# Layer 0 neighbour gather: a GpSimd queue drain behind every one of its 416 indirect DMAs

## The reference, cut to what matters

```python
xn = _layernorm(x)
msgs = edge_weight[:, None] * xn[edge_src]                # 50,000 x 256
agg = jax.ops.segment_sum(msgs, edge_dst, num_segments=3125)
h = (1.0 + eps[0]) * xn + agg
x = x + (jax.nn.relu(h @ w1 + b1) @ w2 + b2)
# then: routed experts, typed attention over the same edges, slice attention
```

## Time and profile before

| | |
|---|---|
| Median of 3 runs | 4517.4 us (4517.17 to 4521.95) |
| The profiled execution, its own time | 4514.77 us |
| Its span from first to last instruction | 4513.0 us |
| POOL busy over the span | 2876.4 us (64%) |
| PE busy | 2845.5 us (63%) |
| DVE busy | 2409.3 us (53%) |
| First gather to the end of the last gather | 592.7 us window |

### The profile page before, as it was taken

How to read it: one execution, slowest core, us unless ns; L and a number is a source line. 1 busy time by engine, 2 the same in 40 slices (tenths; PEclk the granted TensorE clock), 3 DMA queues, 4 the chain that set the end, 5 groups by cost and what they waited for, 6 DMA issues and landing times.

```text
span 4513.0 us, 51523 instructions
## 1 busy us (share of the span) xinstructions
PE 2845.5 (63%) x13735; PEld 1923.5 (43%) x13735; DVE 2409.3 (53%) x5005; ACT 1721.4 (38%) x4345; POOL 2876.4 (64%) x2661
## 2 busy tenths in 40 slices
PE   4200005545473990767777778996777777996698
PEld 1000003333362660224444447884444445885455
DVE  6434434444451114336777775556777776665353
ACT  2222310000021112125555556774555555885451
POOL 4777776666667887665555557996555553555640
PEclk5555556777785995777777778997777778997798
DMA  5444449333345653677676676777887765664300
GB/s 163 134 136 127 141 116 245 91 93 93 89 90 191 196 183 101 212 220 215 202 212 207 203 191 163 204 193 190 208 210 208 209 203 141 173 173 131 102 1 29
DMA packets 805880, 720.83 MB, mean 160 GB/s; under 512 B 424290, under 2 KB 700364, under 8 KB 805469
## 3 DMA queue, kind: packets, MB, share of 16 engines
q1 hardware_dynamic: 645116, 399.08, 31.1%
q0 software_dynamic: 153536, 315.11, 25.1%
q10 hardware_dynamic: 6944, 3.34, 0.3%
HBM read 482.09 MB, written 241.99 MB: 160 GB/s over the span
## 4 chain that ended last, share of the span: by engine, by line
DVE 20%; POOL 16%; another core or an unknown queue 12%; PE 12%; issue 9%; ACT 7%; DVEq 4%; ACTq 2%; DMA 1%; SPq 1%; POOLq 0%
POOL rec_src L564 9%; DVE META L1423 7%; POOL AR L1661 4%; DVE BIGR L648 3%; DVE AR L1443 3%; ACT AR L1717 2%; DVEq L1439 2%; DVE AR L639 2%; DVE AR L1436 2%; ACT AR L1719 1%; ACT AR L1547 1%; PE ps L1822 1%; PE ps L2433 1%; ACTq L1718 1%
## 5 line engine op out<-in xcount | busy, mean ns | idle before, releaser
L1392 POOL DMA_INDIRECT AR<-kv_tab,META x832 | 791.0, 951 | 599.8 <-DVE AR L1436 337.0
L536 POOL DMA_INDIRECT rec_dst<-AR,slot_e x400 | 484.6, 1211 | 166.7 <-issue 166.4
L1423 DVE TENSOR_REDUCE META<-ps 128x8 f32<-128x1024 f32 x416 | 507.7, 1221 | 97.9 <-remote 57.7
L668 PE MATMUL ps<-AR 128*128 128x256 f32 x832 | 305.6, 532 | 362.4 <-issue 151.0
L622 POOL DMA_INDIRECT AR<-xn_tab,META x416 | 397.9, 956 | 199.7 <-issue 128.6
L1661 POOL TENSOR_TENSOR AR<-AR 128x896 f32<-128x896 f32 x208 | 352.1, 1693 | 233.3 <-ACT AR L1726 230.4
L1626 DVE TENSOR_TENSOR BIGR<-BIGR,ps 128x260 f32 x832 | 353.6, 425 | 228.9 <-PE ps L1700 144.6
L1700 PE MATMUL ps<-AR 128*128 128x260 f32 x1664 | 419.5, 395 | 11.3 <-POOL AR L1661 5.4
L1521 PE MATMUL ps<-AR,identb 128*128 128x512 bf16 x832 | 405.4, 487 | 15.4 <-issue 8.5
L564 POOL DMA_INDIRECT rec_src<-AR,slot_e x290 | 351.8, 1213 | 91.8 <-issue 88.3
L668 PEld LDWEIGHTS ps<-AR 128*128 128x128 f32 x832 | 212.8, 268 | 456.1 <-issue 262.3
(11 more groups left out here) (432 smaller groups left out, 5815.7 us busy)
## 6 DMA issues: line engine op xcount, KB each, us to landing
v_dst<-AR SPq DMA_DIRECT2D x104, 384.0 KB
AR<-v_dst SPq DMA_DIRECT2D x104, 384.0 KB
v_src<-AR SPq DMA_DIRECT2D x104, 384.0 KB
AR<-v_src SPq DMA_DIRECT2D x104, 384.0 KB
AR<-in_W_qvk SPq DMA_DIRECT2D x44, 608.0 KB
rec_raw<-AR SPq DMA_DIRECT2D x40, 640.0 KB, 3.3
AR<-rec_dst SPq DMA_DIRECT2D x104, 192.0 KB
AR<-rec_src SPq DMA_DIRECT2D x104, 192.0 KB
```

The source lines that it names most:

```text
L536: pool.indirect_dma_start(rec_tab[0], bass.IndirectOffsetOnAxis(ap=slot_e[0][0:EP, c * CC + k:c * CC + k + 1].bitcast(U32), axis=0), RD[s] ...
L668: ins = pe.matmul(l0_ps(s, u), OW[s][:, u, :], GA[s][:, u, :], start=True, stop=True)
L1392: pool.indirect_dma_start(KVR[s][:, u, 0:KV], None, kv_tab, bass.IndirectOffsetOnAxis(ap=META[o][:, g * U + u, 0:1].bitcast(U32), axis=0)) ...
L1423: ve.tensor_reduce(BMALL[o][:, g * U + 2 * half:g * U + 2 * half + 2, :].rearrange("p b h -> p (b h)"), PSA[:, 2048 + 1024 * half:3072 + 1 ...
```

## The change

`pool.drain()` is put behind each indirect DMA of `l0_pool`, inside the loop over the four blocks of a group. That is 416 drains in all. A drain on an engine's queue holds back what follows it on the same queue until the engine has finished what stands ahead of it. No instruction changes its place, no wait, buffer, semaphore or size changes, and all other stages and engines keep their code.

```diff
@@ -622,6 +622,7 @@
                     pool.indirect_dma_start(GA[s][:, u, :], None, xn_tab,
                                             bass.IndirectOffsetOnAxis(ap=META[0][:, g * U + u, 0:1].bitcast(U32), axis=0)
                                             ).then_inc(sem(f"rows{s}"), 16)
+                    pool.drain()
 
         def l0_vector(ve):
             ve.tensor_tensor(X[:, 0:N2, :], X[:, 0:N2, :], b2x.unsqueeze(1).to_broadcast([P, N2, D]), ALU.add)
```

## The result

The changed kernel takes 5444.2 us (median of 4 runs, 5433.7 to 5451.8) against 4517.6 us before. The ratio is 1.205, with an interval of 1.202 to 1.207. I had forecast 4640 us, with a range that ended at 4705. The time lies at rival B, which I had priced at 5427 us and given a chance of 0.05.

The account below looks back on a forecast made before the run. POOL's gather issue was taken to set the stage's pace, 5.0 of 5.7 us a group. Stage +128.9 us, less 5.4 at its end, on 4514.8 gave 4638.3, stated as 4640 us; range 4595 to 4705.

Parts of the forecast that it names:

- rival B: Drain waits until the gather has landed, gap 2.68 us between POOL's gathers, whole 5427 us; chance 0.05.
- the price of a drain between gathers: On POOL in the gather stage, each gap between gathers grows from 0.30 to 0.78 us; 415 gaps make 323.7 us.
- work ahead: POOL's queue prepares the next gather while the present one runs, starting it 0.30 us after; a drain ends that.
- the sum's 721.6: Forecast gather stage on POOL: 397.9 us busy plus 323.7 us of gaps, against 592.7 us before.
- The price of lost preparation: Next gather on POOL is prepared only after the present one finishes; gap 0.78 us instead of 0.30.
- My sum: Whole-kernel forecast: 128.9 us more for the gather stage less 5.4 at its end, +123.5 us.
- The pauses: POOL's waits for late PE increments in the gather stage, 70.3 us, all to be given back at the slower pace.
- Rival A: POOL's pauses stay despite the slower gathers; up to +55 us, 4695 us, or 4710 with all of it; chance 0.10.
- The end of the stage: POOL resumes 6.3 us after the last gather instead of 11.75, which gives back 5.4 us.
- What follows: Everything after the gather stage starts later by the same time; it costs nothing more and hides nothing.
- The cover: DVE's and PE's 2.8 to 2.9 us per group lie well inside POOL's 6.9 us in the gather stage.

Follow-up runs that it names:

- e3: Kernel before, with a POOL wait for each gather's own landing and a drain behind that wait; 5487.4 us, ratio 1.207.
- e1: Kernel before, with a tiny POOL memset behind each gather and a wait for its semaphore, no drain; 4562.2 us, ratio 1.0035.
- e5: Changed kernel, drains kept, with gathers of 256-byte rows instead of 1 KB; 4929.4 us, ratio 1.206 to the kernel before.
- e6: Changed kernel, drains kept, with gathers of 2 KB rows, each for two blocks; 4457.0 us, ratio 1.091 to the kernel before.
- e7: Kernel before, with a tiny memset, a wait for its semaphore and a nop behind each gather, no drain; 4691.8 us, ratio 1.039.
- e4: Kernel before, with one drain behind the fourth gather of each group only, 104 in all; 4750.6 us, ratio 1.045.

## Why the prediction was wrong

**The step that failed** is the price of a drain between gathers. I bounded it by rows in which work ahead had finished, and took "finished" to be the gather's recorded end. A gather's record ends 1.81 us before its last increment lands, and the drain waits for the landing. e3 (113 ns with nothing in flight), e1 (engine free 0.11 us after the record) and e5 with e6 (the drain follows the length of the transfer) show it. The gap was 2.7 us on average and not 0.78. The stage came to 1522.6 us and not to the sum's 721.6. These 801 us are nearly the whole error of 5444 - 4640 = 804 us.

**The rule that I let weigh too much** is that of the Trainium skill, "PSUM — Partial Sum Buffer", "Engine vs sequencer instructions": a drain waits for the engine to go fully idle. I read it as leaving transfers out. No row spoke for that reading, and with no row on either side a chance of 0.05 was far too low. In these runs POOL's drain counts its own indirect DMAs in flight. It doesn't count those of SP's queue: the zero fills took 14.4, 27.8 and 42.7 us to land, and no drain beside them was longer than 7.5 us. Other engines' drains were not tried.

**Rival B's sum was right.** It took 1.90 us from the earlier trace rows and 0.78 from the earlier trace rows, gap 2.68, whole 5427 us. Measured were a gap of 2.7 and 5444 us. That they agree so closely is partly luck. B's parts are a little long: a single gather's gap in the quiet part of the stage is 2.6 us (1.88 + 0.70). What brings the mean up are the 20 early gathers with slow landings, which B did not price.

**The price of lost preparation was right** where nothing has to land. Behind a drain the next gather starts 0.70 us later, and e7, which has that price without a landing, has 0.75. My sum with e7's memset added is 123.5 + 415 x 0.12 = +173 us; measured were 4691.8 - 4515.8 = +176. The 50 ns that the Trainium skill, "DMA: Bandwidth & Descriptors", section "Anatomy of one DMA — SWDGE (gpsimd) path", gives for the dispatch would have made it far less. By the gaps of 0.75 us in e7 it isn't the time from release to start of a DMA that the queue had not prepared.

**The pauses went,** as forecast: no remote wait is left on POOL, and DVE's adds follow PE's products by 0.14 us. Rival A was wrong. Their 70 us were a gain inside a loss of 930.

**The end of the stage** gave back 11.75 - 7.18 = 4.6 us, forecast 5.4. What follows kept its length, as forecast.

**The cover held.** PE's and DVE's work per group stayed far inside POOL's pace, 14.6 us a group now. PE's rose from 2.9 to 383.2 / 104 = 3.7 us, at a mean granted clock of 0.56 instead of 0.73, and that cost nothing.

## What to carry to other kernels

Behind an indirect DMA on POOL, a drain costs the DMA's whole way to its landing plus the start of the next DMA from nothing: here 2.7 us on top of the engine's 0.95 us of work. To hold the next DMA only until the engine is free, let a tiny POOL instruction increment a semaphore and let the next DMA wait for it (0.38 us between gathers). To order the data, let the DMA that needs it wait for the landing semaphore, which was 0.4 to 0.5 us cheaper for each gather than the drain and can be put several DMAs later, as PE's wait for four gathers is in this kernel. A nop between a wait and a DMA costs nothing while the wait is met early (0.30 us gaps in the kernel before), and some 0.5 us where the queue stands at the wait.

## What the runs showed of the hardware that I had not expected

PE's semaphore increments seem to reach all waiting engines up to 15 us late while POOL issues indirect DMAs back to back. In this stage POOL's pauses came to 69.6 us at a gather each 1.26 us and 25.3 us at 1.34 us; at e1's 1.49 us, and in e4 with its break of 2.8 us after every fourth gather, there were none. In the stage right behind, beside scatters each 1.49 us, DVE's adds were prompt. They were not everywhere beside scatters: where POOL issues one each 1.3 to 1.5 us for `kv_tab` and `qs_tab`, ACT waited 37.7 us for remote releases (L1283, 13 times).

It was not so on each chip. On the one of e5 and e6 no remote wait stands in either trace, the second layer's gather stages, whose code is unchanged, included. The kernel before had, from 1990 to 3780 us, among others:

```profile
ACT AR L1569 <- remote: 457.3, 92, 20.9
DVE AR L1436 <- remote: 240.8, 86, 10.6
```

On that chip the kernel before took 4086.2 us, 431 less than on the first one. There is no trace of the kernel before on it, but e5's shows where most of the time went: from the first to the last of the second layer's 832 gathers it took 1428.6 us, and 1760.7 in the kernel before on the first chip. The mean granted clock of the two stretches differs too, 0.96 against 0.79, and PE was busy 1145.3 against 1370.6 us. Whether the late increments cost that time, or the lower clock, or one brings the other about, no run parts. What holds the increments back stays open.
